# A transformer block in split half precision: the lead and the end of the order reworked, the last FFN's lower parts on one engine

## The reference

```python
x = x + 0.5 * ffn(layernorm(x))
x = x + attention(layernorm(x))     # q, k, v of 16 heads, RMS norm of q and k,
                                    # score bias -distance * slope * softplus(k . u), causal softmax
x = x + 0.5 * ffn(layernorm(x))
# ffn: W1 and W2 each get an addition per batch, the products of the normalised
# even and odd tokens 1 to 16 of that batch, times scale; exact gelu between them
```

## Time and profile before

| | |
|---|---|
| median of three runs | 801.34 us |
| the profiled execution, its own time | 801.33 us |
| its span, first to last instruction | 799.3 us |
| TensorE matmuls busy | 769.1 us, 96%, 9645 of them |
| VectorE, ScalarE, GpSimd busy | 668.3, 655.0, 643.6 us |
| mean granted clock of TensorE | 0.993 |

### The profile page before, as it was taken

The page is one execution under the profiler, slowest core; times in us unless marked ns, Lnnn a source line. Parts: engine busy times, 40 slices in busy tenths (PEclk is TensorE's granted clock), DMA queues, the critical chain, the costliest instruction groups (busy, mean ns, idle before and its releaser), DMA issues.

```text
span 799.3 us, 25575 instructions
## 1 busy us (share of the span) xinstructions
PE 769.1 (96%) x9645; PEld 547.2 (68%) x9645; DVE 668.3 (84%) x1903; ACT 655.0 (82%) x1421; POOL 643.6 (81%) x754
## 2 busy tenths in 40 slices
PE   5889999999999999999999999999999999999996
PEld 2435767677767777677667777677776776677773
DVE  7988787987888888888989878888889779889865
ACT  5849887888988799797998889897997889985763
POOL 5427979888988989789888889889897898886781
PEclk9989999999999999999999999999999999999999
DMA  7162615554265623546162642647244461629320
GB/s 185 18 140 51 147 41 121 82 135 96 43 146 84 148 57 91 121 91 138 29 152 51 134 95 55 141 86 148 59 94 109 107 122 29 160 48 184 46 49 27
DMA packets 97297, 77.12 MB, mean 96 GB/s; under 512 B 71662, under 2 KB 84080, under 8 KB 97176
## 3 DMA queue, kind: packets, MB, share of 16 engines
q1 hardware_dynamic: 96696, 73.92, 43.7%
q10 hardware_dynamic: 480, 1.57, 0.9%
HBM read 4.74 MB, written 2.10 MB: 9 GB/s over the span
## 4 chain that ended last, share of the span: by engine, by line
PE 77%; DVE 7%; ACT 5%; POOL 4%; DMA 3%; issue 2%; SPq 2%; ACTq 0%; DVEq 0%
PE ps L1027 14%; PE ps L1029 13%; PE ps L1028 13%; PE ps L1151 8%; PE ps L1178 7%; PE ps L1179 7%; PE ps L1133 5%; PE ps L1180 3%; POOL qkn L824 2%; DMA qk<-qkn 2%; PE ps L1153 2%; DMA x_in<-in_L_attn_x 1%; POOL pt_l L800 1%; PE ps L1044 1%; ACT qkn L913 1%
## 5 line engine op out<-in xcount | busy, mean ns | idle before, releaser
L800 POOL TENSOR_TENSOR pt_l<-pt 128x512 f16<-128x512 f32 x368 | 322.0, 905 | 58.4 <-ACT pt L987 56.9
L987 ACT ACTIVATE pt<-ps 128x512 f32<-128x512 f32 (+1 forms) x384 | 174.9, 531 | 27.3 <-PE ps L1180 13.9
L1483 DVE CUSTOM_DVE_ANT_0 masked<-ps,causal_row 128x512 f16<-128x512 f32 (+1 forms) x256 | 149.0, 620 | 20.6 <-PE ps L1151 18.1
L824 POOL TENSOR_TENSOR qkn<-qkn,rs 128x512 f32<-128x512 f32 x128 | 129.6, 1042 | 44.1 <-ACT rs L924 44.1
L1178 PE MATMUL ps<-qk 128*128 128x512 f16 (+3 forms) x512 | 146.8, 300 | 0.0
L1179 PE MATMUL ps<-qk 128*128 128x512 f16 (+3 forms) x512 | 146.5, 299 | 0.0
L1027 PE MATMUL ps<-v_buf,pt 128*128 128x65 f16 x1280 | 129.7, 194 | 1.7 <-POOL pt_l L800 1.3
L1028 PE MATMUL ps<-v_buf,pt 128*128 128x65 f16 x1280 | 129.8, 193 | 0.0
L1029 PE MATMUL ps<-v_buf,pt_l 128*128 128x65 f16 x1280 | 129.5, 193 | 0.0
L1027 PEld LDWEIGHTS ps<-v_buf,pt 128*128 128x128 bf16 x1280 | 118.0, 98 | 8.9 <-issue 2.1
L1028 PEld LDWEIGHTS ps<-v_buf,pt 128*128 128x128 bf16 x1280 | 117.5, 98 | 3.2
(11 more groups left out here) (193 smaller groups left out, 2057.3 us busy)
## 6 DMA issues: line engine op xcount, KB each, us to landing
qk<-qkn SPq DMA_DIRECT2D x186, 256.0 KB, 4.0
x_in<-in_L_attn_x SPq DMA_DIRECT2D x8, 256.0 KB, 3.0
out<-x_out SPq DMA_DIRECT2D x8, 256.0 KB, 2.9
qk<-qkn ACTq DMA_DIRECT2D x6, 256.0 KB, 5.2
qk<-qk SPq DMA_DIRECT2D x1, 1024.0 KB, 8.4
qk<-gtt SPq DMA_DIRECT2D x64, 8.0 KB
qk<-nmt SPq DMA_DIRECT2D x64, 2.0 KB
y_hl<-ytt SPq DMA_TRANSPOSE x63, 3.1
```

The lines of the kernel that those rows point to most:

```text
L800: g.tensor_tensor(pt_l[:, h % 2, c], pt[:, h % 2, c], pt_h[:, h % 2, c], ALU.subtract).then_inc(s_pt_l, 1)
L824: g.tensor_tensor(qk, qk, r.unsqueeze(4).broadcast_to([P, 2, 2, 2, D]), ALU.mult).then_inc(s_qkn, 1)
L987: a.activation(pt[:, h % 2, c], ps[:, j, 0:width], ACT.Exp).then_inc(s_exp, 1)
L1483: ins = d.tensor_tensor_reduce(masked[:, part.unit(s, i)[0], col:col + (ib + 1) * P], part.bank(s, i)[:, col:col + (ib + 1) * P], causal_r ...
```

## The change

- A stage "gp" on ScalarE loads GELU's table, in the lead before "zt" of norm a and in the end between "zt" and "m" of the last FFN. The load back behind the last GELU is left out. The other 14 FFNs are as before.
- For the two `shared` FFNs VectorE makes all four `hid_l` and GpSimd none. VectorE takes `od` without waiting for ScalarE's copy, ScalarE's copy waits for `od`, and `zt_l` is subtracted between the adapted W1 and W2.
- In batch 7 the attention's result is written to `x_in` instead of `x_2`, so it needn't wait for the FFN sum of batch 6, which reads `x_2`.
- In batch 0 TensorE adds the causal mask for all token blocks (`masked_by_dve`), and VectorE's maximum is a plain one.
- In `ORDER` nearly every list has entries swapped. In the lead: "setup" ahead of "ln2" and "b2" behind "m" on VectorE; "uu" ahead of the fillers; "wq" 1 and 2 on ScalarE from ahead of attention to between its tiles of q and k, "wol" and "wvl" on GpSimd to between quads 0 and 1; 24 filler matmuls for 32, none of them near the gate's rows; "t" 2 ahead of "gr" 0 and the fourth v tile behind the first maxima; "s" 0 and 1 earlier. In the end: "wp" 2 ahead of the last weighted sum, the output of batch 6's FFN and its residual sum behind "wp" 3, and six fillers behind the last output. The first and body sections swap neighbours, among them "yt" 2 ahead of "pl" 8 on GpSimd.

```diff
     "tensor": {
         "lead": [
-            ("setup", NEXT), ("zt", "a", NEXT), ("m", "a", NEXT), ("warm", 0, 6, NEXT), ("h", "a", NEXT),
-            ("out", "a", NEXT), ("warm", 1, 8, NEXT), ("warm", 1, 10, NEXT), ("zt", "att", NEXT), ("qk", 0, 0, NEXT),
-            ("qk", 0, 1, NEXT), ("qk", 0, 2, NEXT), ("qk", 0, 3, NEXT), ("qk", 1, 0, NEXT), ("qk", 1, 1, NEXT),
-            ("uu", NEXT), ("qk", 1, 2, NEXT), ("qk", 1, 3, NEXT), ("v", 0, 0, NEXT), ("t", 0, NEXT), ("t", 1, NEXT),
-            ("gl", 0, NEXT), ("v", 0, 1, NEXT), ("v", 0, 2, NEXT), ("warm", 0, 8, NEXT), ("v", 0, 3, NEXT),
-            ("gr", 0, NEXT), ("t", 2, NEXT), ("t", 3, NEXT), ("a", 0, NEXT), ("a", 1, NEXT), ("qk", 2, 0, NEXT),
-            ("a", 2, NEXT), ("a", 3, NEXT), ("qk", 2, 1, NEXT), ("qk", 2, 2, NEXT), ("nm", 0, NEXT),
-            ("qk", 2, 3, NEXT), ("a", 4, NEXT), ("a", 5, NEXT), ("qk", 3, 0, NEXT), ("qk", 3, 1, NEXT),
-            ("qk", 3, 2, NEXT), ("a", 6, NEXT), ("s", 0, NEXT), ("a", 7, NEXT), ("qk", 3, 3, NEXT), ("t", 4, NEXT),
...
+            ("setup", NEXT), ("zt", "a", NEXT), ("m", "a", NEXT), ("h", "a", NEXT), ("out", "a", NEXT), ("uu", NEXT),
+            ("warm", 1, 10, NEXT), ("zt", "att", NEXT), ("qk", 0, 0, NEXT), ("qk", 0, 1, NEXT), ("qk", 0, 2, NEXT),
+            ("qk", 0, 3, NEXT), ("qk", 1, 0, NEXT), ("qk", 1, 1, NEXT), ("warm", 0, 6, NEXT), ("warm", 1, 8, NEXT),
+            ("qk", 1, 2, NEXT), ("t", 0, NEXT), ("qk", 1, 3, NEXT), ("t", 1, NEXT), ("v", 0, 0, NEXT),
+            ("gl", 0, NEXT), ("v", 0, 1, NEXT), ("t", 2, NEXT), ("gr", 0, NEXT), ("t", 3, NEXT), ("v", 0, 2, NEXT),
+            ("a", 0, NEXT), ("a", 1, NEXT), ("qk", 2, 0, NEXT), ("a", 2, NEXT), ("a", 3, NEXT), ("qk", 2, 1, NEXT),
+            ("qk", 2, 2, NEXT), ("a", 4, NEXT), ("nm", 0, NEXT), ("v", 0, 3, NEXT), ("qk", 2, 3, NEXT),
+            ("a", 5, NEXT), ("qk", 3, 0, NEXT), ("qk", 3, 1, NEXT), ("qk", 3, 2, NEXT), ("s", 0, NEXT),
+            ("qk", 3, 3, NEXT), ("a", 6, NEXT), ("s", 1, NEXT), ("a", 7, NEXT), ("t", 4, NEXT), ("gl", 1, NEXT),
+            ("nm", 1, NEXT), ("pv", 0, NEXT), ("t", 5, NEXT), ("v", 1, 0, NEXT), ("t", 6, NEXT),
         ],
...
         "final": [
...
-            ("m", "c", LAST), ("s", 14, THIS), ("pv", 13, THIS), ("s", 15, THIS), ("pv", 14, THIS), ("h", "c", LAST),
-            ("pv", 15, THIS), ("wp", 2, THIS), ("yx", THIS), ("out", "c", LAST), ("wp", 3, THIS),
-            ("warm", 2, 6, THIS), ("zt", "c", THIS), ("m", "c", THIS), ("warm", 3, 7, THIS), ("h", "c", THIS),
-            ("out", "c", THIS),
...
+            ("pv", 12, THIS), ("s", 14, THIS), ("pv", 13, THIS), ("s", 15, THIS), ("h", "c", LAST), ("pv", 14, THIS),
+            ("wp", 2, THIS), ("pv", 15, THIS), ("yx", THIS), ("wp", 3, THIS), ("out", "c", LAST), ("zt", "c", THIS),
+            ("m", "c", THIS), ("warm", 3, 7, THIS), ("h", "c", THIS), ("out", "c", THIS), ("warm", 2, 6, THIS),
         ],
...
     "scalar": {
         "lead": [
-            ("ln1", "a", NEXT), ("sel", NEXT), ("wq", 0, NEXT), ("zt", "a", NEXT), ("setup", NEXT), ("wq", 1, NEXT),
-            ("m", "a", NEXT), ("h", "a", NEXT), ("wo", NEXT), ("wq", 2, NEXT), ("ln1", "att", NEXT),
+            ("sel", NEXT), ("ln1", "a", NEXT), ("setup", NEXT), ("wq", 0, NEXT), ("gp", "a", NEXT),
+            ("zt", "a", NEXT), ("m", "a", NEXT), ("h", "a", NEXT), ("wo", NEXT), ("ln1", "att", NEXT),
             ("zt", "att", NEXT), ("qk", 0, 0, NEXT), ("qk", 0, 1, NEXT), ("qk", 0, 2, NEXT), ("qk", 0, 3, NEXT),
-            ("qkn", 0, 0, NEXT), ("qkn", 0, 1, NEXT), ("qk", 1, 0, NEXT), ("qk", 1, 1, NEXT), ("qk", 1, 2, NEXT),
-            ("qk", 1, 3, NEXT), ("v", 0, 0, NEXT), ("t", 0, NEXT), ("qkn", 1, 0, NEXT), ("t", 1, NEXT),
-            ("qkn", 1, 1, NEXT), ("gate", 0, NEXT), ("v", 0, 1, NEXT), ("rows", 0, NEXT), ("v", 0, 2, NEXT),
-            ("v", 0, 3, NEXT), ("t", 2, NEXT), ("t", 3, NEXT), ("rows", 1, NEXT), ("qk", 2, 0, NEXT),
-            ("qk", 2, 1, NEXT), ("qk", 2, 2, NEXT), ("nm", 0, NEXT), ("qkn", 2, 0, NEXT), ("qk", 2, 3, NEXT),
+            ("qkn", 0, 0, NEXT), ("qk", 1, 0, NEXT), ("qkn", 0, 1, NEXT), ("wq", 1, NEXT), ("qk", 1, 1, NEXT),
+            ("wq", 2, NEXT), ("qk", 1, 2, NEXT), ("qkn", 1, 0, NEXT), ("t", 0, NEXT), ("qk", 1, 3, NEXT),
+            ("t", 1, NEXT), ("qkn", 1, 1, NEXT), ("v", 0, 0, NEXT), ("gate", 0, NEXT), ("rows", 0, NEXT),
...
         "final": [
...
             ("yt", 5, THIS), ("s", 14, THIS), ("m", "c", LAST), ("s", 15, THIS), ("yt", 6, THIS), ("h", "c", LAST),
-            ("yx", THIS), ("ln1", "c", THIS), ("zt", "c", THIS), ("m", "c", THIS), ("h", "c", THIS),
+            ("yx", THIS), ("ln1", "c", THIS), ("zt", "c", THIS), ("gp", "c", THIS), ("m", "c", THIS),
+            ("h", "c", THIS),
...
     "vector": {
         "lead": [
-            ("ln1", "a", NEXT), ("b2", NEXT), ("ln2", "a", NEXT), ("zl", NEXT), ("setup", NEXT), ("zt", "a", NEXT),
...
+            ("ln1", "a", NEXT), ("us", NEXT), ("setup", NEXT), ("ln2", "a", NEXT), ("zl", NEXT), ("zt", "a", NEXT),
+            ("m", "a", NEXT), ("b2", NEXT), ("h", "a", NEXT), ("uu", NEXT), ("add", "a", NEXT), ("ln1", "att", NEXT),
+            ("wq", 0, NEXT), ("ln2", "att", NEXT), ("zt", "att", NEXT), ("gu1", NEXT), ("qk", 0, 0, NEXT),
+            ("qk", 0, 1, NEXT), ("qk", 0, 2, NEXT), ("qk", 0, 3, NEXT), ("gu2", NEXT), ("qk", 1, 0, NEXT),
+            ("qk", 1, 1, NEXT), ("qk", 1, 2, NEXT), ("wq", 1, NEXT), ("t", 0, NEXT), ("qk", 1, 3, NEXT),
+            ("gl", 0, NEXT), ("t", 1, NEXT), ("v", 0, 0, NEXT), ("v", 0, 1, NEXT), ("gr", 0, NEXT), ("t", 2, NEXT),
...
         "final": [
...
+            ("zt", "c", LAST), ("pv", 10, THIS), ("pl", 11, THIS), ("m", "c", LAST), ("pl", 12, THIS),
+            ("pv", 11, THIS), ("wp", 1, THIS), ("pl", 13, THIS), ("pv", 12, THIS), ("pv", 13, THIS),
+            ("pl", 14, THIS), ("pl", 15, THIS), ("pv", 14, THIS), ("pv", 15, THIS), ("wp", 2, THIS), ("yx", THIS),
+            ("wp", 3, THIS), ("ln1", "c", THIS), ("ln2", "c", THIS), ("zt", "c", THIS), ("add", "c", LAST),
+            ("m", "c", THIS), ("h", "c", THIS), ("add", "c", THIS),
...
     "gpsimd": {
         "lead": [
-            ("clear", NEXT), ("m", "a", NEXT), ("h", "a", NEXT), ("ul", NEXT), ("wol", NEXT), ("wvl", NEXT),
-            ("qkn", 0, 0, NEXT), ("qkn", 0, 1, NEXT), ("qkn", 1, 0, NEXT), ("qkn", 1, 1, NEXT), ("gate", 0, NEXT),
-            ("qkn", 2, 0, NEXT), ("qkn", 2, 1, NEXT), ("pl", 0, NEXT), ("qkn", 3, 0, NEXT), ("qkn", 3, 1, NEXT),
-            ("gate", 1, NEXT),
+            ("ul", NEXT), ("m", "a", NEXT), ("clear", NEXT), ("qkn", 0, 0, NEXT), ("qkn", 0, 1, NEXT), ("wol", NEXT),
+            ("wvl", NEXT), ("qkn", 1, 0, NEXT), ("qkn", 1, 1, NEXT), ("gate", 0, NEXT), ("qkn", 2, 0, NEXT),
+            ("qkn", 2, 1, NEXT), ("pl", 0, NEXT), ("qkn", 3, 0, NEXT), ("qkn", 3, 1, NEXT), ("gate", 1, NEXT),
         ],
...
         "body": [
...
-            ("pl", 7, THIS), ("pl", 8, THIS), ("yt", 2, THIS), ("pl", 9, THIS), ("yt", 3, THIS), ("pl", 10, THIS),
+            ("pl", 7, THIS), ("yt", 2, THIS), ("pl", 8, THIS), ("yt", 3, THIS), ("pl", 9, THIS), ("pl", 10, THIS),
...
         "final": [
...
-            ("yt", 2, THIS), ("pl", 9, THIS), ("yt", 3, THIS), ("pl", 10, THIS), ("pl", 11, THIS), ("pl", 12, THIS),
-            ("yt", 4, THIS), ("yt", 5, THIS), ("pl", 13, THIS), ("pl", 14, THIS), ("m", "c", LAST), ("pl", 15, THIS),
-            ("yt", 6, THIS), ("h", "c", LAST), ("m", "c", THIS), ("h", "c", THIS),
+            ("yt", 2, THIS), ("pl", 9, THIS), ("yt", 3, THIS), ("pl", 10, THIS), ("pl", 11, THIS), ("yt", 4, THIS),
+            ("pl", 12, THIS), ("pl", 13, THIS), ("yt", 5, THIS), ("m", "c", LAST), ("pl", 14, THIS),
+            ("pl", 15, THIS), ("yt", 6, THIS), ("h", "c", LAST), ("m", "c", THIS),
...
         def alone(n, b):
+        def masked_by_dve(b, ib):
+            return b > 0 and ib >= 2
+        def attended(b):
+            return x_in if b == B - 1 else x_2
         def shifts(n, b):
...
-        def pool_count(n, b, each):
-            before = b * each - (each // 2 if n == "a" and b > 0 else 0)
-            return before
+        def pool_weights(n, b):
+            return 2 * b - (1 if n == "a" and b > 0 else 0)
         def _(sp):
...
             def hidden_lo(part, s, b, n):
-                for r in range(0, FB, 2 if shared(n, b) else 1):
+                if shared(n, b):
+                    return
+                for r in range(FB):
...
+                    if shared(n, b):
+                        act.wait_ge(s_od[n], b + 1)
             def w2_hi(part, s, b, n):
+            def gelu_table(part, s, b, n):
+                act.preload_act_table_set("gelu_and_others")
             def gelu(part, s, b, n):
-                act.preload_act_table_set(EXP_SET)
+                if (n, b) != ("c", B - 1):
+                    act.preload_act_table_set(EXP_SET)
             def take_qk(part, s, b, qd, t):
...
             def normalize(part, s, b, n):
```

(39 more changed lines are left out.)

228 lines of the change are left out of this document (109 added, 119 removed).

## The result

The changed kernel takes 806.15 us (805.49 to 807.63, five runs) where the kernel before takes 800.72: 0.67% slower, 95% interval of the ratio 1.0049 to 1.0085. The profiled execution is the median one: 806.15 us, span 804.1. The forecast of 798.6 (795.0 to 801.8) was wrong in sign.

The account below looks back on a forecast made before the run. TensorE was taken as the bound in six of the eight batches, with idle time at the two ends. From 801.33 us, the end's 2.93 off, masks' 0.9 on and lead's 0.7 off gave 798.6 us, range 795.0 to 801.8.

Parts of the forecast that it names:

- The first FFN: Start of the lead: adapted W1 0.3 us and GELU 1 us sooner, given back by VectorE; 0, 1 us either side.
- The middle of the lead: Between q, k and gate: last gate operation 1.9 us later, but its rows turned at 48.6 for 49.04, 0.4 won.
- Rival D: Lead: the copies moved into its middle are uncovered, lead +2, 801.3 us; chance 0.07.
- End of the lead: Up to 70 us: the first two heads' scores fill part of TensorE's 1.79 us idle time, 0.3 us sooner.
- The masks: Batch 0: TensorE adds masks for two more token blocks, 0.9 us later, 1.8 if none covered; VectorE's maximum unchanged.
- First batch and body: Batches behind the lead: the new order swaps neighbours, TensorE hardly waits, nothing to win; 0.
- Up to the last "wp" 3: Last batch: the last output projection starts 0.9 us earlier (0.1 to 1.4), with its transposing DMA issued sooner.
- GELU's table: Last FFN: loading the table while ScalarE waits for W2 lets GELU start 1.28 us sooner.
- The lower parts on VectorE: Last FFN: VectorE alone makes all four at 693 ns each, 0.75 us sooner; a loss of 1.0 at 1198 ns.
- E: Body: GpSimd's new order makes one head's weighted sum 1.17 us late per batch, 7.0 in all, 805.6 us; chance 0.08.
- B: Lead gives its bound, a gain of 3.3 us, 796.0 us in all; chance 0.25.
- C: End gives half, 1.65 us, through another GELU table load or TensorE's clock falling again: 799.9 us; chance 0.12.

Follow-up runs that it names:

- e14: The changed kernel with VectorE's bias rows and normalised tokens of the first FFN ahead of scaling W1 and W2, GpSimd's clearing before its lower part: 804.57 us.
- e9: The changed kernel with the old first FFN and early weight work, new order behind, u's matmuls in place of the 14 fillers: 801.01 us.
- e15: e9's lead, first and middle batches in the old order with VectorE's mask, and the new end: 798.57 us, ratio 0.9974 to the kernel before.
- e18: e15 with ScalarE's second and third weight copy and GpSimd's two lower parts of weights between the lead's q and k: 799.75 us.
- e11: e1 with TensorE adding batch 0's masks of token blocks 2 and 3: 799.26 us, ratio 0.9979 to the kernel before.
- e4: The changed kernel with VectorE adding the mask of token blocks 2 and 3 in batch 0, as before: 807.84 us.
- e13: The new code in the old order on all engines, without the stage for GELU's table, with VectorE's mask: 800.72 us.
- e1: The new code with the old order in lead, first and middle batches and VectorE's mask, only the end new: 798.29 us, ratio 0.9975 to the kernel before.
- e6: The changed kernel with VectorE's bias rows back ahead of the normalisation and GpSimd's clearing of buffers back at its head: 809.44 us.
- e10: The new first FFN, then the old order of attention in the lead with weight work early, otherwise the changed kernel: 807.94 us.
- e7: The changed kernel with ScalarE's second and third weight copy, VectorE's second lower part and GpSimd's two of weights back ahead of attention's normalised tokens: 805.15 us.
- e2: The changed kernel with the old lists of the lead on all engines: 802.64 us.
- e17: e15 with the new order in the six middle batches only: 800.45 us, ratio 0.9996 to the kernel before.
- e5: The changed kernel with the six filler matmuls ahead of the hidden products of batch 0 put back: 808.25 us.
- e12: e1 without the stage that loads GELU's table early, so the load stands in front of the first GELU again: 798.38 us.
- e8: The changed kernel with GpSimd's old lists in the first and middle batches, other engines keeping their new lists: 812.39 us.
- e16: The changed kernel with one TensorE swap undone in the six middle batches, the sixth head's scores behind one product again: 809.43 us.

## Why the prediction was wrong, step by step

- **The first FFN** ("I find the normalised tokens of attention where they were"). This step failed: first q came 1.7 us late. I let the adapted W1 come 0.3 sooner because W1 and W2 are scaled first, and did not ask when their turned banks are there: VectorE waits 1.64 us for them while the tokens lie ready, and W1 comes at 13.74 for 13.55. I then gave VectorE's added work a gain of 1 us to eat, which did not exist: the bias rows (1.3, and 2.8 beside the memsets) and u (1.9) stand in its path. And I put the six fillers ahead of the hidden products at nothing: without them nine of these products start 0.43 us apart, and GELU is fed late even where the bias rows are gone (the last ends at 21.62 in e14, 20.10 before). e9, which undoes all of it, has the first q at 28.93; no run undoes one part alone and gets more than 0.8 us of it back (e14), so how the 1.7 us divide is not shown.
- **The middle of the lead** (the gate's last operation 1.9 us later, but its rows at 48.6). I had the copies and lower parts, and bounded them by a loss of 1.9, then took a gain of 0.4, as the rows waited 2.4 us for TensorE before. The gate's last operation came at 51.43, 5.1 later: 1.7 from the first q; 1.6 because GpSimd's second quad starts later behind it (the forecast's 1.9, near enough); and 1.8 behind that start, from GpSimd's 2.02 for 1.04 us beside VectorE's subtraction and a wait of 0.78 for ScalarE. e15 has those 1.8 as well (6.8 us from the start of the second quad to the gate's last operation, 6.9 here, 5.1 before), as it too has this subtraction between q and k. TensorE, at half clock behind its wait of 3.14, then turned the rows 1.1 us after they were there; in e15, at full clock, it did so at once. What I left out is that VectorE's two-input work and GpSimd's stand still for each other: I had named that rule for the end and did not apply it to the two 2.13 us and the subtraction that I moved myself. The Trainium skill, SBUF — State Buffer, Who interferes with whom, says that a VectorE instruction with two inputs in SBUF contends with a GpSimd instruction that reads SBUF, and that the one waits out the other; the 3.05 for 1.19, the 0.97 for 0.17 and e18's 2.06 for 0.18 us agree. Rival D, with 0.07, was this stretch (its +2 against 2.1 measured), only it came with the other losses.
- **End of the lead** (0.3 sooner): from the gate's rows to the first placement 14.1 us, 13.3 before, 0.8 later. The bound of a gain of 3.3 for the whole lead was also added up wrongly, its three terms make 3.2; the loss of 4.7 lies outside the other bound, 3.
- **The masks** (+0.9, bounds 0 to 1.8). In the old order 0.6 to 1.5 us by the marks and nothing by the medians (e11), inside the bounds. In the new order TensorE's mask is 1.0 us better in batch 0 (e4). So "I take no change" for VectorE failed there; that VectorE is the scarcer engine of that order is argued, not shown.
- **First batch and body** (0). "There is nothing to win" was right, and I took from it that nothing would be lost. 0.44 us a batch is too small to see in any one row, and six times that is more than the end's GELU term. The sign that I had named for it, TensorE below 89.5 of 90 us, was too coarse: it read 89.70.
- **Up to the last "wp" 3** (-0.9): measured -2.6 in the profile. The size failed. From the store of batch 5 on TensorE is busy 3.7 us less (69.04 for 72.75; the 49 matmuls of the FFN's output, 2.7 us, went behind "wp" 3) and idles 1.0 more (3.5 for 2.5). The transposing DMA is issued 68.70 us behind that store, before 71.81: 3.1 sooner, where I had 1.5, since I took GpSimd's last lower parts to stay where they were. The DMA still ends last (1.62 us of waiting), so the chain that I named is the right one.
- **GELU's table** (-1.28): 0.8. "What is late next" was the step; I checked only the first hidden product, not TensorE's whole work behind it. The trace still shows no drain behind the load: GELU at 788.97, the load at 787.68.
- **The lower parts on VectorE** (-0.75): 0.5 (e13), at 0.62 us each as taken; the last ends 0.80 us behind the last GELU, forecast 0.76, and the last matmul 0.88 behind that, forecast 0.67. With the table loaded early nothing of it is seen in the changed kernel, where TensorE's work ends last (2.2 us behind GELU).
- **Rivals.** E, the one slower case, forecast 805.6, close to the 806.15, and that is luck: it put 7.0 us into the middle batches by GpSimd's order, where 2.5 are, by another wait, and the larger loss is the lead's. B fell with the first FFN. Of C, the fallen clock at the end happens in ten of eighteen profiles, by 0.7 to 1.3 us.

## What to carry to other kernels

Where two or three engines take turns on a path, ask of each moved instruction when its operand is there and what both of its new neighbours do on the other engines: a subtraction of 16 columns cost 2 us because of what GpSimd did beside it. Put work into an engine's wait (the bias rows in a load's shadow) and not behind it. A new order for a stretch in which the bound engine idles 0.3% had only losses to give here, so take the end's lists alone: e1 and e15, with the middle left as it was, are 0.25% faster than the kernel before and 0.9% faster than the changed one. And an edit that undoes one part can create a seam that neither kernel has (e6, e10): look at the trace before its time is read.

## What the runs showed of the hardware

- VectorE's 1x512 tensor_scalar took 1.12 us beside GpSimd's memset and 0.41 without, its 128x16 subtraction up to 2.06 for 0.18: length does not protect an instruction; e18's ended with GpSimd's whole operation. GpSimd is held as well: its 1.04 us operation took 2.02 beside VectorE's subtraction (changed kernel, 44.50), and all eight took 1.04 in e7, where that subtraction stands elsewhere.
- TensorE's granted clock fell to 0.50, 1.2 GHz, behind the waits of 3.14 us (changed kernel, about 46 to 53 us), 2.76 (e15, e18) and 2.07 (e18), and not in the same place in every execution: the same "wp" 3 had 0.70 in e15 and 1.00 in e1, behind the same wait of 1.62.
- The hidden products of the first FFN started 0.43 us apart, twice their 0.22, while the granted clock read 1.00: in all nine profiles without the six fillers ahead of them, and with the fillers in five of eleven (ten products in e2, e9, e13 and e17, four in e5). e12 and e13 have the same fillers and the same wait of 1.01 us, and the pace is 0.22 in the one and 0.43 in the other. The fillers made it rarer and did not prevent it.
- Undoing parts of a changed order one by one made it worse, clear of noise, in five of eleven cases (e4, e5, e6, e8, e16): the lists of the engines fit each other.
